# Graph attention with a layer norm: maxima up to 4 heads ahead, exponentials 2 heads ahead, one projection job per step

## What is computed

```python
q, k, v = (split_heads(x @ W + b) for W, b in (Wq, bq), (Wk, bk), (Wv, bv))   # 12 heads of 32
scores = q @ k.T / sqrt(32) + beta * adj
scores = where(adj > 0, scores, -9e15)
out = softmax(scores) @ v                    # heads joined again: 256 x 384
result = layernorm(x + out)                  # over the 384 features, eps 1e-5
```

## Time and profile before

| | |
|---|---|
| median of 3 runs | 880.39 us (878.81 to 881.38) |
| the profiled execution | 875.0 us |
| its span, first to last instruction | 873.2 us |
| PE busy | 769.3 us (88% of the span) |
| DVE busy | 610.8 us (70%) |
| ACT busy | 592.8 us (68%) |
| POOL busy | 415.4 us (48%) |
| PE share of the chain that ended last | 80%; DVE 10%, issue 7% |
| mean granted TensorE clock | 0.986 of full speed |

### The profile page before, as it was taken

One profiled execution on the slowest core, in us unless ns is written; L12 is line 12 of the kernel. 1 busy time (PEld: TensorE's weight loads), 2 busy tenths in 40 slices (PEclk: granted clock), 3 DMA queues, 4 the chain that ended last, 5 costly groups with the idle time before them and its releaser, 6 DMA issues.

```text
span 873.2 us, 23363 instructions
## 1 busy us (share of the span) xinstructions
PE 769.3 (88%) x7296; PEld 624.9 (72%) x7296; DVE 610.8 (70%) x2391; ACT 592.8 (68%) x2020; POOL 415.4 (48%) x660
## 2 busy tenths in 40 slices
PE   5898999988999989898989898989998988999882
PEld 4776777777777777777777777777777776777751
DVE  3567676767776667777677777677777677677675
ACT  3667676677676667676676776777676667676772
POOL 2423445564445553455544455644455554445533
PEclk9999999999999999999999999999999999999997
DMA  4100011111011110111110111110111110111001
GB/s 150 62 1 21 31 50 50 50 50 32 19 51 49 50 49 3 49 50 50 50 45 7 50 50 49 50 50 2 50 50 50 50 50 8 44 50 50 20 20 37
DMA packets 28537, 37.02 MB, mean 42 GB/s; under 512 B 2560, under 2 KB 28416, under 8 KB 28416
## 3 DMA queue, kind: packets, MB, share of 16 engines
q1 hardware_dynamic: 28416, 35.53, 12.7%
HBM read 22.94 MB, written 12.58 MB: 41 GB/s over the span
## 4 chain that ended last, share of the span: by engine, by line
PE 80%; DVE 10%; issue 7%; ACT 1%; DMA 1%; DVEq 0%; SPq 0%; ACTq 0%
PE j_bank L273 25%; PE t_bank L341 16%; PE s_bank L328 12%; PE j_bank L270 12%; PE j_bank L293 11%; DVE neg_scores L440 4%; DVE probs_t L472 2%; PE j_bank L282 2%; PE j_bank L301 2%; DVE xt_low L455 1%; DVE neg_max L440 1%; DMA beta_col<-in_L_gnn_beta_dram 1%; ACT probs L370 1%; DVEq L430 0%; ACT w_high L404 0%
## 5 line engine op out<-in xcount | busy, mean ns | idle before, releaser
L370 ACT ACTIVATE probs<-neg_scores,neg_max 128x256 f32<-128x256 f32 x768 | 381.6, 499 | 23.4 <-DVE neg_max L440 23.4
L440 DVE CUSTOM_DVE_ANT_0 neg_scores<-s_bank,bias_sb 128x256 f32<-128x256 f32 x768 | 286.7, 419 | 46.1 <-PE s_bank L328 44.7
L341 PE MATMUL t_bank<-ident,probs 128*128 128x128 f32 x1536 | 231.0, 280 | 43.6 <-ACT probs L370 29.4
L341 PEld LDWEIGHTS t_bank<-ident,probs 128*128 128x128 f32 x1536 | 169.0, 141 | 93.9 <-ACT probs L370 89.5
L472 DVE COPY probs_t<-t_bank 128x512 f32<-128x512 f32 x256 | 175.4, 685 | 0.7 <-PE t_bank L341 0.7
L452 DVE TENSOR_SCALAR qk<-j_bank,qk_bias 128x256 f32<-128x256 f32 x96 | 46.4, 484 | 153.4 <-PE j_bank L273 153.4
L370 ACT ACTIVATION_READ_ACCUMULATOR probs<-neg_scores,neg_max 128x1 f32 x768 | 146.3, 190 | 0.0
L273 PE MATMUL j_bank<-xt_high,w_high 128*128 128x256 f32 x576 | 110.1, 300 | 26.0 <-DVE xt_low L455 24.2
L381 ACT ACTIVATE qk<-j_bank,qk_bias 128x256 f32<-128x256 f32 x96 | 45.7, 476 | 124.1 <-PE j_bank L273 124.1
L328 PE MATMUL s_bank<-qk 32*128 32x256 f32 x1536 | 110.4, 401 | 0.9 <-DVE neg_max L440 0.9
L664 POOL TENSOR_SCALAR o_sb<-y_sb,rstd,shift 128x384 f32<-128x384 f32 x62 | 102.6, 1662 | 9.7 <-POOL shift L659 9.7
(11 more groups left out here) (53 smaller groups left out, 945.8 us busy)
## 6 DMA issues: line engine op xcount, KB each, us to landing
x_sb<-in_x_dram SPq DMA_DIRECT2D x32, 384.0 KB, 3.7
out_dram<-o_sb SPq DMA_DIRECT2D x31, 384.0 KB, 2.8
adj_sb<-in_adj_dram SPq DMA_DIRECT2D x32, 256.0 KB, 4.0
w_raw<-in_L_gnn_Wq_dram SPq DMA_DIRECT2D x1, 576.0 KB, 4.6
w_raw<-in_L_gnn_Wk_dram SPq DMA_DIRECT2D x1, 576.0 KB, 6.5
w_raw<-in_L_gnn_Wv_dram SPq DMA_DIRECT2D x1, 576.0 KB, 8.1
out_dram<-o_sb SPq DMA_DIRECT2D x2, 192.0 KB, 1.9
bv_row<-in_L_gnn_bv_dram SPq DMA_DIRECT2D x1, 192.0 KB, 4.8
```

What stands on the lines that cost most here:

```text
L341: mm = pe.transpose(b[:, k * N + t * P:k * N + (t + 1) * P], probs[:, (T * s + t) % (T * NH), k * P:(k + 1) * P], ident[:, :])
L370: nc.scalar.activation(probs[:, slot, :], neg_scores[:, slot, :], ACT.Exp, bias=neg_max[:, n % 2, t, h:h + 1], scale=-1.0, accum_out=row_s ...
L440: nc.vector.tensor_tensor_reduce(neg_scores[:, (T * s + t) % (T * NH), :], s_bank[h % J][:, t * N:(t + 1) * N], bias_sb[:, n % 2, t, :], - ...
```

## The change

The change rewrites the order of all three engines' streams and leaves every computation as it is.

- `probs` becomes a ring of `NX` = 8 heads (before: 4), `neg_scores` stays at 4. ScalarE's step s now copies head s (before: s - 1), then runs the exponentials of head s + 2 (before: s + 1), then reads out the step's own jobs.
- VectorE's maxima run three heads ahead; the last step of a group runs those of s + 3 and of s + 4, and the first step of a group none. It copies head s in step s. Both `moments` move to step 8, where `gather_moments` stands, and `seed` to step 9.
- TensorE runs a group's `scores` in the first step of the group before it (h % 4 is 0, before: 2), then that step's O job, and only then the step's `turn`.
- `jobs_of` has one or two jobs in each step, in a new order.

```diff
     def jobs_of(n, h):
         jobs = {
-            0: (("Q", 0, n + 1), ("K", 0, n + 1)),
-            1: (("O", 2, n - 1),),
-            3: (("G", 2, n - 1), ("Q", 1, n + 1), ("K", 1, n + 1)),
-            4: (("Q", 2, n + 1), ("K", 2, n + 1)),
-            5: (("O", 0, n),),
-            7: (("G", 0, n), ("V", 0, n + 1), ("X", 0, n + 2)),
-            8: (("V", 1, n + 1), ("X", 1, n + 2)),
-            9: (("O", 1, n),),
-            11: (("G", 1, n), ("X", 2, n + 2)),
+            0: (("O", 2, n - 1),),
+            1: (("Q", 0, n + 1),),
+            2: (("G", 2, n - 1), ("K", 0, n + 1)),
+            3: (("V", 0, n + 1),),
+            4: (("O", 0, n),),
+            5: (("X", 0, n + 2), ("Q", 1, n + 1)),
+            6: (("G", 0, n), ("K", 1, n + 1)),
+            7: (("V", 1, n + 1),),
+            8: (("O", 1, n),),
+            9: (("X", 1, n + 2), ("Q", 2, n + 1)),
+            10: (("G", 1, n), ("K", 2, n + 1)),
+            11: (("X", 2, n + 2),),
         }.get(h, ())
...
             for n in range(B):
                 for h in range(H):
-                    if h % J == 2:
+                    if h % J == 0:
                         if h < H - J:
                             scores(n, h // J + 1)
                         elif n + 1 < B:
                             scores(n + 1, 0)
+                        for job in jobs_of(n, h):
+                            run(job)
                     turn(H * n + h)
-                    for job in jobs_of(n, h):
-                        run(job)
+                    if h % J != 0:
+                        for job in jobs_of(n, h):
+                            run(job)
...
-                    if s + 1 < B * H:
-                        exps(s + 1, 0)
-                    for job in rest_of(n, h - 1):
+                    if by_scalar(h):
+                        copy_turned(s)
+                    if s + 2 < B * H:
+                        exps(s + 2)
+                    for job in jobs_of(n, h):
                         take(job)
...
+                    if h % J != 0 and s + 3 < B * H:
+                        maxima(s + 3)
+                    if not by_scalar(h):
+                        copy_turned(s)
+                    if h % J == 3 and s + 4 < B * H:
+                        maxima(s + 4)
...
-                    if h in (6, 7) and n >= 1:
-                        moments(n - 1, h - 6)
                     if h == 8 and n >= 1:
+                        for t in range(T):
+                            moments(n - 1, t)
                         gather_moments(n - 1)
-                    if h == 10 and n >= 1:
+                    if h == 9 and n >= 1:
                         seed(n - 1)
```

More of the change, by code:

```diff
@@ L108, in graph_attention_program @@
         neg_max = sb("neg_max", [P, 2, T, H])
[L109 removed]
+        probs = sb("probs", [P, T * NX, N])
         row_sum = sb("row_sum", [P, 2, T, H])
@@ L363, in _, with exps @@
         def _(act):
-            def exps(s, t):
+            def exps(s):
                 n, h = s // H, s % H
[L366 to L372, removed]
+                wait(act, turned, s - NX + 1)
+                for t in range(T):
+                    act.wait_ge(max_ready, T * s + t + 1)
+                    nc.scalar.activation(probs[:, (T * s + t) % (T * NX), :], neg_scores[:, (T * s + t) % (T * NH), :],
+                                         ACT.Exp, bias=neg_max[:, n % 2, t, h:h + 1], scale=-1.0,
+                                         accum_out=row_sum[:, n % 2, t, h:h + 1]).then_inc(exp_ready, 1)
             def take(job):
@@ L406, in _ @@
                 take(job)
-            for t in range(T):
-                exps(0, t)
+            for h in range(2):
+                exps(h)
             for n in range(B):
@@ L411, in _ @@
                     s = H * n + h
-                    if s + 1 < B * H:
-                        exps(s + 1, 0)
-                    for job in rest_of(n, h - 1):
-                        take(job)
-                    if s + 1 < B * H:
-                        exps(s + 1, 1)
-                    if s >= 1 and by_scalar((s - 1) % H):
-                        copy_turned(s - 1)
-                    for job in first_of(n, h):
-                        take(job)
-            if by_scalar(H - 1):
-                copy_turned(B * H - 1)
+                    if by_scalar(h):
[3 more added lines that the diff above has]
+                    for job in jobs_of(n, h):
+                        take(job)
             take(last_jobs[0])
@@ L562, in _ @@
                 take(job)
-            for s in range(2):
+            for s in range(J):
                 maxima(s)
@@ L567, in _ @@
                     s = H * n + h
-                    for job in rest_of(n, h - 1):
-                        if job[0] == "K":
-                            take(job)
-                    if h % J != 2 and s + 2 < B * H:
-                        maxima(s + 2)
-                    if s >= 1 and not by_scalar((s - 1) % H):
-                        copy_turned(s - 1)
-                    for job in rest_of(n, h - 1):
-                        if job[0] == "X":
-                            take(job)
-                    if h == 1 and n + 1 < B:
+                    if h % J != 0 and s + 3 < B * H:
[4 more added lines that the diff above has]
+                        maxima(s + 4)
+                    if h == 0 and n + 1 < B:
                         edges(n + 1)
-                    if h % J == 2:
-                        if h > J:
+                    if h % J == 0:
+                        if h > 0:
                             invert(n, h // J - 1)
@@ L584, in _ @@
                             invert(n - 1, G - 1)
-                    if h in (6, 7) and n >= 1:
-                        moments(n - 1, h - 6)
                     if h == 8 and n >= 1:
+                        for t in range(T):
+                            moments(n - 1, t)
                         gather_moments(n - 1)
-                    if h == 10 and n >= 1:
+                    if h == 9 and n >= 1:
                         seed(n - 1)
-                    if h % J == 2 and s + 2 < B * H:
-                        maxima(s + 2)
-                    for job in first_of(n, h):
+                    for job in jobs_of(n, h):
                         take(job)
-            if not by_scalar(H - 1):
-                copy_turned(B * H - 1)
             invert(B - 1, G - 1)
```

9 lines of the change are left out of this document (2 added, 7 removed).

## The result

The changed kernel takes 1028.5 us, the median of four runs from 1023.1 to 1039.1; the kernel before, beside it, 879.6. The ratio is 1.167 with a 95% interval of 1.158 to 1.177: slower, as forecast. The median is 31 us above the 997 of the forecast, above the 970 to 1022 that the forecast had by itself, and 3.5 us under the upper end of the range. The ratio leaves out the slowest of the four runs (1039.1 us, clock 0.926), which is the one profiled; the other three have a median of 1023.3 us and clocks of 0.931 to 0.947.

A forecast was written before the change was run, and what follows sets the result against it. TensorE was taken as the bound: 22.9 us of work plus seven waits make 30.05 a graph against 26.28; 29 graphs by 3.77, with ends of 5.9 and 2, add 117, for a median of 997 us, range 950 to 1032.

The forecast's parts named there:

- The period: One middle graph on TensorE: 22.9 us of work plus seven waits gives 30.05 us, against 26.28 before.
- The scores' waits (2.1, 0.8, 0.2): Scores wait for VectorE's maxima: 2.1 us after K2, 0.8 after V0, 0.2 after V1.
- G's wait in step 10 (1.9): G waits 1.9 us for X1's bank, which VectorE reads after copies, statistics and maxima.
- Q1's wait for O's bank (1.45): Steps 4 and 5: Q1 waits 1.45 us, as ScalarE reads O only after copying head 4 and the exponentials.
- K0's and G's: K0 loses 0.5 us waiting for Q0's bank; G in steps 6 to 8 loses 0.2 until X0 is read.
- The ends (5.9 and 2): Start and end of the run: graph 1's Q0 comes 5.9 us later, the last two graphs add 2.
- the clock rival: TensorE's clock falls in each graph around the 1.9 and 2.1 waits, costing 1.5 us each: 1042 us; chance 0.10.
- The vector rival: VectorE is not behind at step 10, so G waits 0.4 us, not 1.9: 952 us; chance 0.12.
- the two on the faster side: Only the scores' waits remain, 875 us, chance 0.05; or all seven waits go, 783 us, chance 0.03.
- What would show it: Signs in the profile after: scores' waits some 90 us in all, G waiting about 1.9 for `xt_low`, Q0 every 30 us.

The follow-up runs named there:

- e4: Changed kernel plus nine thrown-away matmuls before the transposes of head 10 and nine more before X2; 999.5 us, ratio 1.136.
- e1: Changed kernel, but in a group's last step VectorE runs the maxima of both heads before copying the head's transposes; 993.9 us, ratio 1.131.
- e5: Changed kernel with the next group's scores moved to the head of a group's second step; 891.3 us, ratio 1.013.
- e2: Changed kernel with the statistics of the graph before moved from step 8 to the end of step 7; 985.5 us, ratio 1.120.
- e3: Changed kernel, but in step 4 ScalarE reads O before copying head 4 and running the exponentials; 1023.1 us, ratio 1.162.
- e13: Changed kernel, but ScalarE reads each step's jobs before the exponentials, and in a group's first step also before the copy; 982.7 us, ratio 1.121.
- e10: Changed kernel plus only nine thrown-away matmuls, before the transposes of head 10; 1020.4 us, ratio 1.164.
- e6: Changed kernel with scores in the second step, statistics in step 7, ScalarE's reads first, VectorE's copy before maxima in a group's last step; 823.5 us, ratio 0.937.
- e11: e6 with the exponentials one head ahead in place of two; 1053.0 us, ratio 1.201.

## Why the prediction was right, and what it left out

- *The period.* Right. Against 30.05, graphs at full clock take 29.96, and e4, where all graphs run at full clock, has a mean of 30.01 and 999.5 us against 997.
- *The scores' waits (2.1, 0.8, 0.2).* Right in size, and shown by e1 (two of them shortened by 0.6 each, 1.23 measured) and by e5, which removes them.
- *G's wait in step 10 (1.9).* Right; 2.0 in the timeline, and e2 shows that the statistics make up most of it (1.46 of the period).
- *Q1's wait for O's bank (1.45), and K0's and G's.* Right in size. e3 shows a limit of adding such terms: removing the largest alone gave back 0.27 of 1.45, as the next bank was released late by the same cause. e13 removes the cause.
- *The ends (5.9 and 2).* Both too small. The Q0 of graph 1 and that of graph 30 in e4, and that of graph 30 before:

```profile
61.96 0.59 PE L270 MATMUL j_bank<-xt_high,w_high 128*128 128x256 f32 x3
...
931.94 0.60 PE L270 MATMUL j_bank<-xt_high,w_high 128*128 128x256 f32 x3
...
814.07 0.59 PE L273 MATMUL j_bank<-xt_high,w_high 128*128 128x256 f32 x3 [0.94 <-DVE xt_low L455]
```

Here 61.96 is 8.0 after the 53.99 of before (0.6 of it is there at the first scores, before anything that changed), and from 931.94 to the end of the span (996.1) are 64.2 us, where before it was 59.1 (from 814.07 to 873.2): 5.0 more. The profiled execution of e4, 997.9 us, is thus 6 above the forecast 992. That the medians, 999.5 and 997, are only 2.5 apart is luck: the 5.4 added for the median over the profiled execution was 1.6 in e4.

- *The order of chances.* The forecast and the clock rival were put down as excluding each other, and the rival had 0.10. Both happened: the walk holds, and on top of it 28 us by the ratios (1.167 against the 1.136 of e4) are lost to the clock. So the verdict and the waits came out as forecast, but the median lies above the forecast's own 1022, in the part of the range that was there for the clock rival. The sum of the forecast has no term for the clock's fall. The rival's "each graph pays 1.5" was too much: the mean graph pays 1.3 in the profiled execution, and the 28 us are 0.9 for each graph. I had argued against it with the few falls of the kernel before, but there two pauses of 1.0 and 1.07 stand with a transpose between; here the pauses are twice as long. K's matmuls between them did not protect: e10 and e2 have falls with only one of the two pauses left long.
- *The vector rival, and the two on the faster side.* Wrong as forecasts, each needs a wait to hide that does not. But what they priced was there to be had: the 1.5 of the vector rival is the 1.46 of e2, and e6, which takes nearly all the waits away, is at 823.5, between the 875 and the 783.
- *What would show it.* The scores' waits came to 75.6 in all where some 90 were named, since a slow clock hides part of them (87.2 in e10, whose clock is 0.964); the wait for `xt_low` stood there as "issue".

The Trainium skill (Perfetto Trace Analysis, Matmul Optimizations) has TensorE scale its power with its use and wants matmuls back to back. Taken as the granted clock, e4 bears that out: matmuls thrown away into the waits raise it from between 0.93 and 0.95 to between 0.98 and 0.99, and the run is 28 us shorter by the ratios. The Trainium skill (Perfetto Trace Analysis, Optimizing Tensor Performance, Matmuls) rotates banks so that reading one out overlaps the next matmuls. That is true of e6 and not of the changed kernel, where Q1 waits 1.28 and G 1.88 for a bank, with the same two banks: what differs is the order in which the engines come to their reads and to the scores.

## What to carry to other kernels

In streams of fixed order, a look-ahead is slack, and here it helped only where the work that others wait for (reads that free a bank) ran before the work that was brought ahead; the same look-ahead and table stand here in a kernel of 1028 us and in one of 823. Price each release from both sides: what the releasing engine still has to do, and what the waiting one has to do meanwhile, over every step of the loop and not at two of them. And when waits of 2 us are predicted on TensorE, give the clock a term of its own: here it was 28 us beside the 110 or so of the waits.

## What the runs showed of the hardware

- The clock's price can be near that of a wait. In the changed kernel a fall lasted up to ten microseconds, and the mean graph lost 1.3 us to it in the profiled execution. Two pauses of 2.0 us in each graph brought it down (0.93 to 0.95 in the mean), and so did one of 2.0 with the other at 0.4 or 0.8 (0.958 in e2, 0.964 in e10). Pauses of 1.3 and 0.7 in each graph did not (e5, 0.988), nor did three of 1.54 with shorter ones between (e11, 0.989), and nine matmuls in each of the two pauses kept it up (e4, 0.989).
- The four runs of the changed kernel spread over 16 us (1023 to 1039), and the clock with them (0.947 to 0.926). A clock that falls does not have to mean such a spread: e13, at 0.943 to 0.948, lies between 982 and 984, and e10, at 0.962 to 0.967, between 1019 and 1021.
- A releaser in the profile is a guess by time: 18.8 us stood under ScalarE's `v_sb` and were VectorE's maxima (e1), and 55.2 us stood under "issue" and were VectorE's X read (e2).
